# A feed-forward pass with its products five steps ahead, loading and layer norm inside it, and every engine loop written out, in a fused transformer block

## The chip, the cores and the metric

The kernel runs on one core of one Trainium2 chip. Its time is the device time of one launch in microseconds (us), the median of three runs. The engines are named as in the profile: PE is TensorE, DVE is VectorE, ACT is ScalarE, POOL is GpSimd, SP is SyncE, which here only issues DMAs.

## The reference

x is 2 x 1024 tokens of 128 channels. Two feed-forward passes stand around one attention:

```python
def ffn(x):                                   # x is layer-normed
    scores = sigmoid(x @ gate_w) + gate_bias  # 8 experts in 4 groups
    # group score: sum of its 2 scores; keep 2 groups, then the 2 best experts in them
    w = 2.5 * chosen / (sum of the 2 chosen + 1e-20)
    experts = silu(x @ w_gate[e]) * (x @ w_up[e]) @ w_down[e]      # I = 64
    shared = silu(x @ sw_gate) * (x @ sw_up) @ sw_down             # I = 128
    return (sum of w[e] * experts[e]) + shared

def attention(x):                             # 16 heads of 8 channels
    q, k, v = split(x @ W_attn + b_attn)
    s = q k^T over all keys;  s = (s - mean(s)) / (mean(|s - mean(s)|) + 1e-6) * 4
    r = relu(causally masked s) ** 4
    return (r / (sum(r) + 1e-6) @ v) @ W_proj + b_proj

x = x + 0.5 * ffn(layernorm(x))
x = x + attention(layernorm(x))
return x + 0.5 * ffn(layernorm(x))
```

## The kernel before, in words

Tokens are cut into 16 tiles of 128, four spans of 512 (four tiles each). The stages follow one another as blocks, with all engines meeting between blocks: loading x with its statistics (`load_x`), first feed-forward pass ("f1"), q, k and v, attention, its merge, and the second pass ("f2"). Inside a block each engine has its own list of instructions, in the order in which the Python code issues them, and runs it strictly in that order; semaphores (`wait_ge`, `then_inc`) tie the lists together. No scheduler moves anything.

A feed-forward pass (`ffn`) holds its hidden layer with hidden channels on the partitions. The eight experts are four chunks of two experts each (128 hidden channels); the shared expert is a fifth. So each of the four spans has five chunks, in the order 0 to 3 and then the shared one. One chunk is: on TensorE the gate product (line 463) and the up product (467), 128 x 512 each; on ScalarE silu of the gate product (588); on VectorE their product (689, `product`), into one of three `hid` buffers; on TensorE the spreading of the token's expert weights over the hidden channels (474, `spread`), which the shared chunk doesn't have; on VectorE the scaling with them (717); on TensorE the down product (446, `down`), which adds five chunks up in one PSUM bank. Gate, up and spread have two PSUM buffers each. In a span TensorE issues for chunk c: products of c, spread of c, down of c-1. After the span ScalarE takes the sum out (573), TensorE turns it back (455, four transposes), VectorE adds it to x (`add_to_x`, 697) and, in f1, takes the statistics for the next norm (310, 319).

Ahead of this stands the routing. TensorE turns the normed x (387), multiplies with the router weights (508, `logits`, two spans at a time), ScalarE takes the sigmoid (557), TensorE turns the scores (519), VectorE adds the bias (643, `scores`) and works out the two experts of each token by counting better ones: `pick_groups` (652 to 662), `pick_experts` (to 669), `weigh` (673 to 681), which ends in `parts`, three bf16 parts of each weight. They are done for span 0 alone first (`now`), and for spans 1 to 3 (`later`) between the chunks of span 0. TensorE turns `parts` (482) and ScalarE takes them as `wT` (577), which `spread` reads. ScalarE loads another function table between sigmoid and silu. Span 0 is written out; spans 1 to 3 are a hardware loop (`Fori`, from line 543 on TensorE).

In f1 the norm of all 16 tiles is one step (`norm_vector`, tiles at 351; every fourth tile on ScalarE, 366), and GpSimd prepares constants for the attention (`attention_constants`, large memsets) beside it. In f2 the first two spans are normed before the block.

The attention runs through eight "quads". Quads 0 and 7 are written out and quads 1 to 6 are a hardware loop over three pairs (`quads`, line 980), on all engines. In a quad TensorE fills a PSUM bank with scores (1048), VectorE masks (1136) or sums (1144), ScalarE and GpSimd (1206) square.

## Time and profile before

| | us |
|---|---|
| median of 3 runs | 505.78 (505.57 to 507.81) |
| span of the profiled execution, whose own time is some 0.4 more (505.8) | 505.4 |
| loading x and statistics | 0 to 9.4 |
| first feed-forward pass | 9.7 to 92.5 |
| q, k, v | 92.7 to 118 |
| attention | 118 to 406 |
| merge | 406 to 431 |
| second feed-forward pass | 431.1 to 502.6 |
| last stores | to 505.4 |
| PE / DVE / ACT / POOL busy | 441.9 (87%) / 402.7 (80%) / 342.0 (68%) / 243.8 (48%) |

A row of a timeline has the start, the duration, the engine, the line of the kernel, the operation with what it writes and reads, how many such instructions stand together, and in brackets how long the engine had been idle and what it waited for. In a row of a chain the first number is the time, the second how much of the chain that step takes. A row of the view by stretches has the stretch, its length, and then the busy time (with the number of instructions) of PE, PEld, DVE, ACT and POOL.

### The profile page before, as it was taken

How to read it: one execution, taken by the hardware profiler on the slowest of the kernel's cores; microseconds unless marked ns; L12 is line 12 of the kernel's file. 1: busy time of each engine (PE TensorE's matmuls, PEld its weight loads, DVE VectorE, ACT ScalarE, POOL GpSimd, SP SyncE). 2: the span in 40 equal slices, each digit the busy share in tenths (PEclk: the TensorE clock that was granted, in tenths of full speed). 3: DMA queues.
4: the chain of work that ended last, by engine and by line, in shares of the span. 5: the costliest groups of instructions: out<-in, count | busy, mean ns of one | idle time of the engine just before them, and what ended most of it. 6: DMA issues, size and time to landing. Idle time of an engine off the chain costs nothing. (4 is left out here: it accounts for less than half of the span.)

```text
span 505.4 us, 8943 instructions
## 1 busy us (share of the span) xinstructions
PE 441.9 (87%) x2736; PEld 168.3 (33%) x2736; DVE 402.7 (80%) x832; ACT 342.0 (68%) x576; POOL 243.8 (48%) x180
## 2 busy tenths in 40 slices
PE   0879999664799999999999999999999995879996
PEld 0323444431232332333333322323323354334442
DVE  5884556976898998999989899989988969784443
ACT  3413223554999999999999999999989931523221
POOL 5940000333777686776877677676876720000000
PEclk9979999975999999999999999999999998799999
DMA  4300000025714205105114124043002300000001
GB/s 118 75 1 0 1 0 0 6 65 127 208 33 78 60 1 95 43 1 93 42 30 71 34 51 84 0 72 63 0 0 50 85 12 0 1 1 0 21 21 42
DMA packets 17796, 21.32 MB, mean 42 GB/s; under 512 B 4748, under 2 KB 10476, under 8 KB 17772
## 3 DMA queue, kind: packets, MB, share of 16 engines
q1 hardware_dynamic: 17452, 20.95, 19.2%
q8 instruction: 12, 0.20, 0.2%
q10 hardware_dynamic: 320, 0.07, 0.1%
q14 instruction: 12, 0.10, 0.1%
HBM read 13.02 MB, written 7.86 MB: 41 GB/s over the span
## 5 line engine op out<-in xcount | busy, mean ns | idle before, releaser
L1206 POOL TENSOR_TENSOR arena<-arena 128x1024 f32<-128x1024 f32 (+1 forms) x120 | 204.0, 1722 | 63.7 <-ACT arena L1178 63.5
L1136 DVE SCALAR_TENSOR_TENSOR arena<-bank,masks 128x1024 f32<-128x1024 f32 (+1 forms) x160 | 174.9, 1114 | 28.9 <-PE bank L1048 28.6
L1178 ACT ACTIVATE arena<-arena 128x1024 f32<-128x1024 f32 (+1 forms) x160 | 148.5, 961 | 8.8 <-DVE arena L1136 5.8
L1048 PE MATMUL bank<-Q,K 128*128 128x512 bf16 (+3 forms) x384 | 91.4, 334 | 10.6 <-DMA K<-k_parts 9.2
L1048 PE MATMUL bank<-K,Q 128*128 128x512 bf16 (+3 forms) x384 | 90.4, 331 | 11.6 <-DVE arena L1136 11.5
L1144 DVE TENSOR_SCALAR_CACHE_REDUCE bank<-bank 128x128 f32<-128x128 f32 (+7 forms) x128 | 94.8, 772 | 0.0
L1168 ACT ACTIVATE bank<-bank 128x128 f32<-128x128 f32 (+7 forms) x128 | 80.9, 632 | 8.9 <-PE bank L1048 8.6
L1079 PE MATMUL bank<-arena,Vq 128*32 128x512 f32 (+3 forms) x768 | 79.6, 495 | 0.0
L588 ACT ACTIVATE arena<-bank 128x512 f32<-128x512 f32 x40 | 23.9, 597 | 76.5 <-PE bank L463 76.5
L689 DVE TENSOR_TENSOR arena<-arena,bank 128x512 f32<-128x512 f32 x40 | 27.4, 686 | 42.8 <-PE bank L467 42.7
L1079 PE MATMUL bank<-arena,ones_rows 128*32 128x512 f32 (+3 forms) x640 | 61.1, 473 | 0.0
L1048 PEld LDWEIGHTS bank<-Q,K 128*128 128x128 bf16 x384 | 26.4, 98 | 95.8 <-issue 42.2
L1048 PEld LDWEIGHTS bank<-K,Q 128*128 128x128 bf16 x384 | 32.5, 98 | 46.3 <-DVE arena L1136 28.1
L446 PE MATMUL bank<-arena,WD 128*128 128x512 f32 x80 | 42.8, 617 | 2.7 <-DVE arena L717 2.6
L463 PE MATMUL bank<-xnT,WG 128*128 (+1 forms) x80 | 42.4, 612 | 2.0 <-ACT arena L577 2.0
L467 PE MATMUL bank<-xnT,WU 128*128 (+1 forms) x80 | 41.7, 604 | 0.0
L1182 ACT ACTIVATE arena<-arena 128x1024 f32<-128x1024 f32 (+1 forms) x40 | 38.9, 972 | 1.3
L917 POOL TENSOR_TENSOR X<-X,bp 128x2048 f32<-128x2048 f32 x1 | 4.5, 4533 | 63.8 <-DVE arena L351 63.8
L1079 PEld LDWEIGHTS bank<-arena,Vq 128*32 128x32 f32 x768 | 17.3, 108 | 35.5 <-issue 34.3
L717 DVE TENSOR_TENSOR arena<-arena,bank 128x512 f32<-128x512 f32 x32 | 22.0, 688 | 5.4 <-PE bank L474 2.2
L1079 PEld LDWEIGHTS bank<-arena,ones_rows 128*32 128x32 f32 x640 | 15.5, 108 | 30.4 <-issue 30.1
L1168 ACT ACTIVATION_READ_ACCUMULATOR bank<-bank (+1 forms) x128 | 23.6, 184 | 0.0
(122 smaller groups left out, 355.4 us busy)
## 6 DMA issues: line engine op xcount, KB each, us to landing
Q<-q_parts SPq DMA_DIRECT2D x24, 192.0 KB
att<-arena SPq DMA_DIRECT2D x28, 128.0 KB, 2.0
K<-k_parts SPq DMA_DIRECT2D x16, 128.0 KB
K<-k_parts SPq DMA_DIRECT2D x8, 192.0 KB
X<-in_L_attn_x SPq DMA_DIRECT2D x4, 256.0 KB, 4.6
K<-k_parts SPq DMA_DIRECT2D x16, 64.0 KB
out_x<-X SPq DMA_DIRECT2D x4, 256.0 KB, 2.3
q_parts<-arena SPq DMA_DIRECT2D x3, 256.0 KB
```

What stands on the lines that cost most here:

```text
L446: mm = nc.tensor.matmul(down_ps, m.WD[:, c, :], hid[:, HID[c], :], start=(c == 0), stop=(c == NCH))
L463: nc.tensor.matmul(gate_ps[c % 2], m.WG[:, c * P:(c + 1) * P], x, start=True, stop=True)\
L467: nc.tensor.matmul(up_ps[c % 2], m.WU[:, c * P:(c + 1) * P], x, start=True, stop=True)\
L689: nc.vector.tensor_tensor(hid[:, HID[c], :], silu[:, c % 2, :], up_ps[c % 2], ALU.mult)\
L1048: last = nc.tensor.matmul(bank[:, lo + shift:hi + shift], left[par][:, g, blk * P:(blk + 1) * P], right[par][:, g, s0:s0 + hi - lo], start ...
L1079: mm = nc.tensor.matmul(acc[32 * g:32 * (g + 1), s0:s0 + hi - lo], w, src, start=start, stop=stop, skip_group_check=True)
L1136: nc.vector.scalar_tensor_tensor(Y(r, g)[:, lo - off(r):hi - off(r)], tiles[slot["lower", r, g]][:, lo:hi], 0.0, mask, ALU.max, ALU.mult). ...
L1144: last = nc.vector.tensor_scalar(src, src, 0.0, 0.0, ALU.max, ALU.add, accum_out=m.upper[:, blk, bass.ds(q * G + g + N_HEAD, 1)])
L1168: last = nc.scalar.activation(src, src, ACT.Relu, accum_out=m.upper[:, blk, bass.ds(q * G + g + N_HEAD, 1)])
L1178: nc.scalar.activation(z, Y(r, g)[:, tile_low(r) - off(r):T - off(r)], ACT.Square)\
L1182: nc.scalar.activation(z, z, ACT.Square).then_inc(fourth_a, 1)
L1206: nc.gpsimd.tensor_tensor(z, z, z, ALU.mult).then_inc(fourth_p, 1)
```

## The change

In both feed-forward passes the shared chunk comes first (ORDER), products run five chunks ahead (AHEAD) into six `hid` buffers, and the first five products are woven into the routing. All 20 chunks are written out. In f1, loading and statistics of x go into the block of the pass; the norm goes span by span; the weights' DMAs stand right behind those of x; GpSimd's attention constants wait for all routing weights. In the attention the loop over quads becomes plain Python, that is straight code.

```diff
+AHEAD, NHID = 5, 6
+ORDER = [NCH, 0, 1, 2, 3]
...
             logits(0)
+            products(0)
             for i in HALVES[1]:
                 norm_transpose(nc, m, s, pe, i)
             turn_scores(0)
+            products(1)
             logits(1)
-            products(0, 0, False)
+            products(2)
             turn_scores(1)
-            products(0, 1, False)
+            products(3)
+            products(4)
             pe.wait_ge(parts_ready, 1)
             turn_weights(0)
             pe.wait_ge(wT_ready, 1)
-            span(0, True)
-            pe.wait_ge(wT_ready, NSPAN)
-            with pe.Fori(1, NSPAN) as i:
-                span(i, False)
-            down(NSPAN - 1, NCH, False)
-            turn_back(NSPAN)
+            for n in range(LAST):                 # 20 chunks
+                if n == 4:
+                    pe.wait_ge(parts_ready, 2)
+                    for j in range(1, NSPAN):
+                        turn_weights(j)
+                    pe.wait_ge(wT_ready, NSPAN)
+                if routed(n):
+                    spread(n)
+                if n + AHEAD < LAST:
+                    products(n + AHEAD)
+                if n and not routed(n):
+                    turn_back(span_of(n) - 1)
+                down(n)
...
         @block.scalar                             # after sigmoid(1)
+            for n in range(AHEAD):
+                gate(n)
+            act.wait_ge(wT_zeroed, 1)
+            take_weights(0)
+            for n in range(LAST):
+                if n == 4:
+                    for j in range(1, NSPAN):
+                        take_weights(j)
+                if n and not routed(n):
+                    take_out(span_of(n) - 1)
+                if n + AHEAD < LAST:
+                    gate(n + AHEAD)
+                if following is not None and n == LAST - AHEAD - 1:
+                    nc.scalar.activation(m.table[:, :], m.eps[:, :], ACT.Sqrt)
+                    act.wait_ge(following.moments_ready, 1)
+                    norm_root(nc, m, following, act, 0)
...
         @block.gpsimd
             if beside is not None:
-                pool.wait_ge(wT_zeroed, 1)
+                pool.wait_ge(parts_ready, 2)
                 beside(nc, m, sem, pool)
...
         @block.vector
+            if start is not None:                 # f1
+                start.moments(dve, 0, s)
+                for i in range(NSPAN):
+                    if i + 1 < NSPAN:
+                        start.moments(dve, i + 1, s)
+                    norm_vector(nc, m, s, dve, i)
             scores(0)
             pick_groups(now)
+            product(0)
             pick_experts(now)
+            product(1)
             scores(1)
             weigh(now)
-            product(0, 0)
+            for n in range(2, AHEAD):
+                product(n)
+            for n in range(LAST):
+                if routed(n):
+                    scale(n)
+                # pick_groups, pick_experts, weigh of `later` at n = 0, 1, 2
+                if n + AHEAD < LAST:
+                    product(n + AHEAD)
+                if place_of(n) == 1 and n > 1:
+                    add_to_x(span_of(n) - 1)      # f1: statistics and moments with it
...
     def quads(engine, body):
-        body(0, 0, 1)
-        with engine.Fori(0, NQUAD // 2 - 1) as pair:
-            body(2 * pair + 1, 1, pair + 1)
-            body(2 * pair + 2, 0, pair + 2)
-        body(NQUAD - 1, 1, NQUAD // 2)
+        for q in range(NQUAD):
+            body(q, q % 2, q // 2 + 1)
```

TensorE at the start of the first pass; L387 (now L408) turns x, L508 (L524) is `logits`, L519 (L535) `turn_scores`, L463 and L467 (L472, L476) the products, L482 the turning of the weights. Before:

```order
L387 MATMUL bank<-ident,arena 128x128 x8
L508 MATMUL bank<-xnT,gw 32x512 x2
L387 MATMUL bank<-ident,arena 128x128 x8
L519 MATMUL bank<-ident,arena 128x64 x4
L508 MATMUL bank<-xnT,gw 32x512 x2
L463 MATMUL bank<-xnT,WG 128x512
L467 MATMUL bank<-xnT,WU 128x512
L519 MATMUL bank<-ident,arena 128x64 x4
```

And now:

```order
L408 MATMUL bank<-ident,arena 128x128 x8
L524 MATMUL bank<-xnT,gw 32x512 x2
L472 MATMUL bank<-xnT,WG 128x512
L476 MATMUL bank<-xnT,WU 128x512
L408 MATMUL bank<-ident,arena 128x128 x8
L535 MATMUL bank<-ident,arena 128x64 x4
L472 MATMUL bank<-xnT,WG 128x512
L476 MATMUL bank<-xnT,WU 128x512
L524 MATMUL bank<-xnT,gw 32x512 x2
```

Two chunks' products stand ahead of the second half of the logits, where none stood; f2 has the same rows but for the first eight transposes.

TensorE at the end of the second pass, with waits; L474 (L484) is `spread`, L446 (L499) `down`, L455 (L509) the turning back. Before:

```order
L463 MATMUL bank<-xnT,WG 128x512 [waits f2_silu]
L467 MATMUL bank<-xnT,WU 128x512 [waits f2_prod]
L443 REGISTER_ALU
L446 MATMUL bank<-arena,WD 128x512 [waits f2_hid]
L543 REGISTER_ALU
L543 COMPARE_AND_BRANCH
L446 MATMUL bank<-arena,WD 128x512 [waits f2_prod]
L455 MATMUL bank<-ident,arena 128x128 [waits f2_y]
```

And now:

```order
L499 MATMUL bank<-arena,WD 128x512 [waits f2_y,f2_prod]
L484 MATMUL bank<-arena,sel 128x512 [waits f2_scaled]
L499 MATMUL bank<-arena,WD 128x512 [waits f2_scaled]
L484 MATMUL bank<-arena,sel 128x512 [waits f2_scaled]
L499 MATMUL bank<-arena,WD 128x512 [waits f2_scaled]
L484 MATMUL bank<-arena,sel 128x512 [waits f2_scaled]
L499 MATMUL bank<-arena,WD 128x512 [waits f2_scaled]
L484 MATMUL bank<-arena,sel 128x512 [waits f2_scaled]
L499 MATMUL bank<-arena,WD 128x512 [waits f2_scaled]
L509 MATMUL bank<-ident,arena 128x128 [waits f2_x,f2_y]
```

The last chunks' products have moved away to places five chunks earlier; spread and down alternate.

VectorE in the attention, where quads 1 to 6 begin, with waits; L1136 (L1186) is the mask step. Before:

```order
L1136 SCALAR_TENSOR_TENSOR arena<-bank,masks 128x512 [waits lower_ready]
L1144 TENSOR_SCALAR bank,upper<-bank 128x512 [waits upper_ready]
L1136 SCALAR_TENSOR_TENSOR arena<-bank,masks 128x512 [waits lower_ready] x2
L1144 TENSOR_SCALAR bank,upper<-bank 128x512 [waits upper_ready]
L984 UNCONDITIONAL_BRANCH
L984 ISA
L1130 ISA [waits relu_round_summed]
L1134 ISA [waits square_done]
L1136 SCALAR_TENSOR_TENSOR arena<-bank,masks 128x1024 [waits lower_ready]
L1130 REGISTER_ALU [waits relu_round_summed]
L1134 REGISTER_ALU [waits square_done]
```

And now:

```order
L1186 SCALAR_TENSOR_TENSOR arena<-bank,masks 128x512 [waits lower_ready] x2
L1194 TENSOR_SCALAR bank,upper<-bank 128x512 [waits upper_ready]
L1186 SCALAR_TENSOR_TENSOR arena<-bank,masks 128x1024 [waits lower_ready,square_done,relu_round_summed] x2
L1194 TENSOR_SCALAR bank,upper<-bank 128x1024 [waits upper_ready]
L1186 SCALAR_TENSOR_TENSOR arena<-bank,masks 128x1024 [waits lower_ready,square_done,relu_round_summed] x2
```

The waits that stood in register instructions of their own have moved onto the instruction, as quad 7 already had them.

## Rows read from the trace of the kernel before

**Rows 1.** Head of the page
```profile
span 505.4 us, 8943 instructions
```

**Rows 2.** Chain that ended last, in order of time, one chunk and the turn back (start, us, what)
```profile
488.07 0.86 PE bank L463 x2
...
489.78 0.22 PE bank L474
490.00 0.86 PE bank L446 x2
490.86 0.44 PE bank L455 x4
```

**Rows 3.** Busy time by stretch: us, busy (x count) per engine, PEclk, DMA share, GB/s
```profile
25.00:30.00 5.00, 2.52 (x10) 0.90 (x10) 3.83 (x12) 1.38 (x3) 4.80 (x16) 1.00 0.00 2
30.00:35.00 5.00, 4.37 (x7) 1.85 (x6) 4.58 (x23) 0.18 (x1) 1.43 (x5) 0.52 0.00 0
```

**Rows 4.** Timeline of the first feed-forward pass (start us, us, engine line op out<-in)
```profile
3.80 0.87 DVE L310 BATCH_NORM_STATS2 stats<-X 128x6 f32<-128x128 f32 x4 [3.80 <-DMA X<-in_L_attn_x]
...
10.41 9.95 DVE L351 TENSOR_SCALAR arena<-X,mv,arena 128x128 f32<-128x128 f32 x12
...
21.38 0.29 DVE L643 TENSOR_TENSOR arena<-bank,gb 128x32 f32<-128x32 f32 x2 [1.02 <-PE bank L519]
```

**Rows 5.** Timeline, start of the second feed-forward pass
```profile
431.11 1.92 PE L508 MATMUL bank<-xnT,gw 128*32 128x512 f32 x4 [3.62 <-PEq L992]
...
435.59 0.29 DVE L643 TENSOR_TENSOR arena<-bank,gb 128x32 f32<-128x32 f32 x2 [2.22 <-PE bank L519]
...
437.08 0.59 ACT L557 ACTIVATE arena<-bank 64x512 f32<-64x512 f32 x1 [1.51 <-PE bank L508]
437.26 0.21 DVE L652 TENSOR_TENSOR arena<-arena 128x28 f32<-128x28 f32 x1
...
438.99 0.60 ACT L588 ACTIVATE arena<-bank 128x512 f32<-128x512 f32 x1
...
439.47 0.29 DVE L643 TENSOR_TENSOR arena<-bank,gb 128x32 f32<-128x32 f32 x2 [0.25 <-PE bank L519]
...
441.56 0.39 PE L482 MATMUL bank<-identb,arena 128*24 128x128 bf16 x4 [0.29 <-DVE arena L681]
...
442.69 0.61 PE L474 MATMUL bank<-arena,sel 128*128 128x512 bf16 x2 [0.74 <-ACT arena L577]
443.19 0.69 DVE L717 TENSOR_TENSOR arena<-arena,bank 128x512 f32<-128x512 f32 x1 [1.08 <-PE bank L474]
...
443.93 1.12 PE L446 MATMUL bank<-arena,WD 128*128 128x512 f32 x2 [0.63 <-DVE arena L717]
...
454.50 1.82 ACT L577 ACTIVATE arena<-bank 24x512 bf16<-24x512 bf16 x3 [0.59 <-PE bank L482]
```

**Rows 6.** Timeline, end of the second feed-forward pass
```profile
500.61 0.60 ACT L573 ACTIVATE arena<-bank 128x512 f32<-128x512 f32 x1 [2.24 <-PE bank L446]
```

**Rows 7.** Timeline of the first pass: TensorE at its loop's start, VectorE's last operation
```profile
44.93 1.12 PE L463 MATMUL bank<-xnT,WG 128*128 x2 [1.11 <-ACT arena L577]
...
92.07 0.38 DVE L319 BATCH_NORM_AGGREGATE mv<-stats 128x2 f32<-128x6 f32 x4
```

**Rows 8.** GpSimd's round-4 squares in quads 4, 5, 6 and 7
```profile
297.02 3.04 POOL L1206 TENSOR_TENSOR arena<-arena 128x512 f32<-128x512 f32 x3 [1.04 <-ACT arena L1178]
...
332.61 3.04 POOL L1206 TENSOR_TENSOR arena<-arena 128x512 f32<-128x512 f32 x3 [1.04 <-ACT arena L1178]
...
368.21 3.04 POOL L1206 TENSOR_TENSOR arena<-arena 128x512 f32<-128x512 f32 x3 [1.04 <-ACT arena L1178]
...
404.26 3.03 POOL L1206 TENSOR_TENSOR arena<-arena 128x512 f32<-128x512 f32 x3 [1.09 <-ACT arena L1178]
```

**Rows 9.** VectorE, the mask step that waits for the same fill, quads 6 and 7
```profile
350.45 1.23 DVE L1136 SCALAR_TENSOR_TENSOR arena<-bank,masks 128x1024 f32<-128x1024 f32 x1 [0.44 <-PE bank L1048]
...
386.39 1.23 DVE L1136 SCALAR_TENSOR_TENSOR arena<-bank,masks 128x1024 f32<-128x1024 f32 x1 [0.54 <-PE bank L1048]
```

More of the change, by code:

```diff
@@ L348, in norm_vector, with norm_tiles @@
         .then_inc(s.rstd_ready, 1)
-    for t in range(t.start, t.stop):
+def norm_tiles(nc, m, s, dve, first, last):
+    for t in range(first, last):
         if t % TPS < TPS - 1:
@@ L388, in norm_transpose, with ffn @@
     last.then_inc(s.xt_ready, 1)
-def ffn(nc, m, sem, tag, beside=None, load=None, following=None, out=None, s=None):
+AHEAD, NHID = 5, 6
+ORDER = [NCH, 0, 1, 2, 3]
+def ffn(nc, m, sem, tag, s, start=None, load=None, beside=None, following=None, out=None):
     a = Arena(m)
     b = m.psum
-    normed = NSPAN // B if s is not None else 0
-    s = s or layer_norm(nc, m, sem, tag, a, [b[0][:, 0:SPAN], b[1][:, 0:SPAN]])
-    part = len(s.parts) - 1
+    normed = 0 if start is not None else NSPAN // B
     tile8 = lambda k=E: a.take(NT * k).rearrange("p (n e) -> p n e", n=NT)
@@ L484, in turn_weights @@
                 last.then_inc(wt_ready, 1)
-            def span(i, first):
-                for c in range(HCH):
-                    again = not first or c >= 2
-                    if again:
-                        products(i, c, True)
-                    if c < NCH:
-                        spread(i, c, again)
-                    if first and c == 4:
-                        pe.wait_ge(parts_ready, 2)
-                        for j in range(1, NSPAN):
-                            turn_weights(j)
-                    if c >= 1:
-                        down(i, c - 1, first)
-                    elif not first:
-                        down(i - 1, NCH, False)
-                    if c == 1 and not first:
-                        turn_back(i)
             def logits(half):
@@ L550, in _ @@
                     norm_transpose(nc, m, following, pe, i)
+            turn_back(NSPAN - 1)
         @block.scalar
@@ L605, in _ @@
                     norm_last_tile(nc, m, following, act, i)
+            take_out(NSPAN - 1)
+            if following is not None:
                 for i in range(NSPAN // B):
                     norm_take(nc, m, following, act, i)
-        if load is not None:
+        if start is not None:
             @block.sync
             def _(sp):
+                start.sync(sp)
                 load(sp)
@@ L709, in span @@
-            def span(i, first):
-                for c in range(HCH):
-                    h = hid[:, HID[c], :]
-                    if not (first and c == 0):
-                        product(i, c)
-                    if c < NCH:
-                        dve.wait_ge(prod_ready, i * HCH + c + 1)
-                        dve.wait_ge(spread_ready, i * NCH + c + 1)
-                        nc.vector.tensor_tensor(h, h, spread_ps[c % 2], ALU.mult).then_inc(hid_ready, 1)
-                    if first and c == 0:
-                        pick_groups(later)
-                    if first and c == 1:
-                        pick_experts(later)
-                    if first and c == 2:
-                        weigh(later)
-                    if c == 2 and not first:
-                        add_to_x(i)
@@ L727, in _ @@
-            span(0, True)
-            with dve.Fori(1, NSPAN) as i:
-                span(i, False)
-            if following is not None:
-                for n in range(NSPAN // B):
-                    last = span_moments(nc, m, dve, n, stats_ready)
-                last.then_inc(following.moments_ready, 1)
-                for n in range(NSPAN // B, NSPAN - 1):
-                    span_moments(nc, m, dve, n, stats_ready)
-                norm_vector(nc, m, following, dve, 0)
-            add_to_x(NSPAN)
@@ L738, in _ @@
-            if out is None:
-                span_moments(nc, m, dve, NSPAN - 1, stats_ready)
+            for n in range(2, AHEAD):
+                product(n)
+            for n in range(LAST):
+                if routed(n):
+                    scale(n)
+                if n == 0:
+                    pick_groups(later)
+                if n == 1:
+                    pick_experts(later)
+                if n == 2:
+                    weigh(later)
+                if n + AHEAD < LAST:
+                    product(n + AHEAD)
+                if place_of(n) == 1 and n > 1:
+                    add_to_x(span_of(n) - 1)
+                if following is not None and n == LAST - 4:
+                    norm_scales(nc, m, following, dve, 0)
+                if following is not None and n > LAST - 4:
+                    half = NSPAN // B * TPS
+                    k = n - LAST + 3
+                    norm_tiles(nc, m, following, dve, [0, 3, 6][k], [3, 6, half][k])
```

297 lines of the change are left out of this document (165 added, 132 removed).

## The prediction

> **What bounds the kernel now.** I read the head of the page first: a span of 505.4 us [rows 1]; the execution's own time is some 0.4 more, so my sum, made against the span, is as good as one against the median of 505.78. Then the chain that ended last, through the second pass. The reader is to see there that inside a span of 512 tokens only TensorE speaks: a chunk is gate and up (0.86), spread (0.22), down (0.86), and once a span the turning back (0.44) [rows 2]. Each row is one step (x2 are the two instructions of one fp32 product), so a chunk is 2.80, and 2.58 without spread. In that steady state nothing is to be gained by looking further ahead: TensorE never waits. What can be gained or lost lies at the two ends of each pass, where the timelines show waits: the routing at the start [rows 4, 5] and the last takings out [rows 6, 7]. The attention, 288 us, is another loop; of it only the code's form changes.
>
> **Second pass, start.** Before: logits(0) begin at 431.11, scores(0) 435.59, pick_experts 437.26, scores(1) 439.47, weights turned at 441.56; sigmoid(1) runs at 437.08 and silu(0) follows at 438.99 [rows 5], that is 1.32 us after the sigmoid's end: a change of function tables.
> Now gate and up of chunk 0 stand ahead of the transposes. The pass begins with TensorE at half clock (the logits took 1.92 for what later takes 1.5; the other half-clock stretch, granted 0.52, is shown in [rows 3]), and before it stayed there until 436.4. So I price chunk 0's products at 2 x 1.72 = 3.44: 433.0 to 436.5. Transposes 0.9, scores turned 0.4: scores(0) at 437.95, 2.4 later than 435.59. Then products of chunk 1 (1.72) and logits(1) (1.5) at full clock: sigmoid(1) at 441.1, 4.0 later, and silu(0) at 443.0, 4.0 later. That is what decides: VectorE's list now has product(0) ahead of pick_experts. scores(0) and pick_groups take 437.26 - 435.59 = 1.67, so VectorE is free at 439.6 and idle until product(0) can run at 443.6. Behind it are queued pick_experts (437.26 to 439.2: 1.95), product(1) (0.63), scores(1) 0.32, weigh (439.8 to 441.5: 1.7): parts at 448.2 to 448.9, against 441.5. I take 448.9: **7.4 later**. Who waits for them: TensorE with turn_weights, and before it products 3 and 4, which wait for silu buffers, which wait for VectorE's product(2), just behind weigh. With 0.35 for turning, 0.6 for taking wT, and product(2) and up(4) between, the loop over chunks begins at 451.6. By then 5 chunks' products are done.
>
> **Second pass, middle.** n = 0 to 3: 4 x 1.72 + 4 x 0.86 + 3 x 0.22 = 10.98, and some 1.3 lost behind pick_experts and weigh of the later spans, each of which holds VectorE 2 to 3 us at a time (an estimate: three spans' worth, against 1.95 and 1.7 for one, in as many instructions): 463.9. Then three turned weights (0.5) and three takings of 0.61 each, 1.82 in all [rows 5], for which the whole loop waits: 466.2. n = 4 to 14 have the full work: 11 x 2.80 minus 2 spreads (0.44) plus 2 turnings (0.88) = 31.24: 497.4. Before, the same three takings lay at 454.5 to 456.3 and three looped spans followed.
>
> **Second pass, tail.** From n = 15 on no products are left. down(15) stands behind turn_back, which waits for take_out (down 14 to its end 1.0, take 0.60 [rows 6]): 2.15 instead of 0.86, 499.6. For n = 16 to 19 TensorE has spread(n), down(n) alone, and down waits for the scaling. From the one place where before shows this naked: spread at 442.69, scaling at 443.19 for 0.69, down at 443.93 [rows 5]: 1.24, and down takes 0.86: 2.10 a chunk, where the same work costs 1.08 when covered. The second spread buffer doesn't help, since spread(n+1) is issued behind down(n). 4 x 2.10 = 8.4: last down ends at 508.0. Before take_out began at 500.61 [rows 6], so **+7.4** for the pass. Bounds: if product(0)'s wait were only 2 us long and the first products not at half clock, parts come 3.5 instead of 7.4 later: +3.5; if TensorE's pauses of over 1 us in the tail bring the clock down (TensorE stood at 0.52, the 1.2 GHz level, in the 5 us after a stretch in which it was busy 2.52 of 5 us [rows 3]), the last 8 us become up to 12: +11.
>
> **First pass.** Here something is really saved. Before, the 12 norm operations took 9.95 beside GpSimd's memsets, 0.83 each [rows 4]; the memsets move behind the routing, so I price them at 0.27 (an estimate from VectorE's other plain fp32 operations on 128 columns or so in [rows 5], 0.2 to 0.3, where GpSimd rests), and they are spread between the statistics, which begin at 3.80. VectorE then needs 4 x (0.91 + 0.29) statistics, 4 x 0.4 and 12 x 0.27: norm of span 3 is done at about 14.2 instead of 20.4. The x transfers land as before; the weights come earlier (their DMAs no longer wait for a new block), in time for gate(0) at 14.0 if they take the 4 us that they took before. logits(0) to 14.0, chunk 0's products to 15.7, transposes to 16.6, scores(0) at 17.2 against 21.38: **4.2 earlier**. Then the same in-order wait as above: sigmoid(1) 20.4, silu(0) 22.3, VectorE idle 4 us, parts at 28.1, where the casts of weigh (0.6 beside GpSimd) now cost 0.2. Before, parts were ready at 28.6. So of the 4.2 only 0.5 is left at this point. The loop begins at 30.9; n = 0 to 3 with later routing and taking of weights to 45.4. Before, at 44.93 TensorE began span 1 [rows 7]; now it has products 0 to 8 and downs 0 to 3 done at 45.4: the same work short of one spread. n = 4 to 14: 31.24 and twice 0.82, since statistics (0.92 + 0.33) stand ahead of the next scaling on VectorE: 78.3. n = 15: take_out stands behind silu(19), a table load and a root on ScalarE, 81.2. n = 16 to 19: 2.1, 3.0 (statistics and norm scales in front), 2.1, 2.1: 90.4 (with some 0.1 rounding). Take out, turn, add, statistics, moments: 94.0, against 92.45 [rows 7]: **+1.6**.
> TensorE's clock: before, it was granted 0.52 from 30 to 35 behind the thin stretch 25 to 30 [rows 3], and the 44.93 has that in it. My steps from 14.0 on are all at 2.4 GHz, and TensorE now has a pause of its own from 20.2 to 22.9. If half clock follows, 5 us of it do 2.6 us of work and cost 2.4, where no wait for VectorE covers them: **+2.4**. Bounds: 0 (no such stretch, or all of it beside waits for VectorE) and 4 (a longer one).
>
> **GpSimd.** The 21 us of constants now run beside n = 3 to 11 of f1; VectorE's operations there read PSUM, and its one routing piece left, weigh(later), is before. Hidden; if not, 0.6 instead of 0.2 on a few operations, under 2 us. If they ended after the pass, q, k, v would wait: 41 + 21 = 62, far from 92.
>
> **Attention.** Rounds of the same kind are 35.59 apart where the loop jumps back between them (297.02 to 332.61), 35.60 where it doesn't (332.61 to 368.21), and 36.05 into quad 7, which is straight code (404.26) [rows 8]. The mask step shows where it goes: idle 0.44 before it in the loop, 0.54 in quad 7 [rows 9]; three waits on one instruction instead of two done ahead in registers. Six quads x 0.45 = **+2.7**. Bounds: 0, if quad 7 is slow for what is last about it (no next quad's loads), and 3.5, if K's loads shift as well.
> A rule against this: the Trainium skill (Runtime: NRT & Kernel Launch, section Instruction fetch mechanics) says that a taken branch breaks the sequential prefetch and that full unrolling is to be preferred. The trace of this case shows 35.59 with the jump back and 35.60 without, so the jump has no price here that its removal could give back. By the rule alone the 2.7 would be 0 or a gain; that outcome is rival 1.
>
> **Sum.** 7.4 + 1.6 + 2.4 + 2.7 = 14.1: a span of 519.5, and a time of about the same. I predict **519.5 us**.
>
> **Rivals.** (1) The straight attention costs nothing: 519.5 - 2.7 = 516.8. For it: one quad is the only witness, and it is also the last. 15%.
> (2) The clock: pauses in both tails and the idle VectorE stretch in f2 give further half-clock stretches, 3 to 6 us more: 522 to 525. For it: [rows 3]; against it, at most one such stretch in each pass before. 20%.
> (3) The front of f2 loses less (product(0) waits 2 us, full clock): 508 to 512. 10%.
> (4) Faster: five products ahead keep TensorE busy through the routing. The place is the start of the pass: before, TensorE was at span 1's start at 44.93 [rows 7] and at 456.7 in f2 with waits of some 10 us in each pass. If product(0) did not hold pick_experts (silu(0) early enough, i.e. before 440 in f2 and 19 in f1), the five products would fill those waits: f1 -8 and f2 -5, with +2.7 for the attention: 495.5. It decides for this side as soon as silu(0) comes less than 1 us after pick_groups ends. Against it: sigmoid(1) and the table load stand ahead of silu(0) on ScalarE, and logits(1) ahead of that on TensorE behind two products. 10%.
> The forecast itself has 45%, its own range 515 to 522.
>
> Under 0.5% (2.5 us) nothing can be told from no change here. Faster: 0.10; same: 0.02; slower: 0.88. The range that leaves out no more than 2 in 10 reaches from 508 to 525.
>
> **What would show it.** Right: in f2 an idle stretch of VectorE of about 4 us between pick_groups and product(0), ended by ScalarE's silu; weights turned at about 449; four spreads at 2.1 us intervals at the end; 36.0 us between quads. In f1 norm operations of 0.27 and scores(0) at about 17. Wrong: a product(0) that starts right behind pick_groups, spreads 1.1 apart in the tail, or quads still 35.6 apart. If the weights' DMAs behind x land after 17 us, f1's start is later and the sum for it too low.

## The result

The changed kernel takes 528.50 us (median of 4 runs, 527.78 to 528.98) against 506.17: a ratio of 1.0436 (1.0414 to 1.0458). It is slower by 22 us. I had predicted slower, 519.5, within 508 to 525: the direction was right, and the time lies 3.5 us outside the range. One execution of x4 below (1472.51 us) and one of x12 (515.0) were slow ones: they stand in no ratio, though the medians below count them.

The page of the profile after has the span:

```profile
span 526.9 us, 7795 instructions
```

It is 21.5 longer than before [rows 1]. These executions took 1.9 to 2.0 us more than their span. The table ahead of the prediction puts this difference at 0.4 for the kernel before; in every execution of it for which both are on record it is 1.8 to 1.9, and those with a span of about 505.4 took 507.0 to 507.4. So 519.5 as a span would have been some 521.4 as a time, an estimate from these differences: of the 9.0 us by which the time was missed, about 2 lie there and 7 in the span. Where the 21.5 arise, by the start of the same operation in both timelines:

| stage | before | after | change |
|---|---|---|---|
| to the first matmul of q, k, v | 92.76 | 99.83 | +7.1 |
| q, k, v, to the first copy of V | 25.6 | 24.9 | -0.7 |
| attention, first to last copy of V | 263.3 | 267.8 | +4.5 |
| to the first logits of the second pass | 49.5 | 49.2 | -0.3 |
| second pass, to its last addition | 70.8 | 81.8 | +10.9 |

**First pass, start** (the timeline, as in [rows 4]):

```profile
11.89 0.85 DVE L372 TENSOR_SCALAR arena<-X,mv,arena 128x128 f32<-128x128 f32 x3
...
18.10 0.29 DVE L684 TENSOR_TENSOR arena<-bank,gb 128x32 f32<-128x32 f32 x2 [4.30 <-PE bank L535]
...
21.54 1.28 ACT L623 ACT_TABLE_LOAD   x1
22.83 1.08 ACT L623 ACTIVATE arena<-bank 128x512 f32<-128x512 f32 x2
...
23.52 0.69 DVE L731 TENSOR_TENSOR arena<-arena,bank 128x512 f32<-128x512 f32 x1 [3.79 <-issue]
```

Three norm operations take 0.85, 0.28 each, where twelve took 9.95. scores(0) come 3.3 us earlier. And then VectorE stands idle for 3.79 us in front of product(0), behind a sigmoid, a table load and silu. TensorE turns the weights at 30.99, later than the 28.62 of the kernel before.

**First pass, tail** (TensorE's timeline, and the busy time by stretches):

```profile
83.49 1.12 PE L499 MATMUL bank<-arena,WD 128*128 128x512 f32 x2 [0.85 <-DVE arena L740]
...
86.30 2.07 PE L499 MATMUL bank<-arena,WD 128*128 128x512 f32 x2 [1.47 <-DVE arena L740]
...
89.65 2.08 PE L499 MATMUL bank<-arena,WD 128*128 128x512 f32 x2 [0.85 <-DVE arena L740]
...
93.00 2.07 PE L499 MATMUL bank<-arena,WD 128*128 128x512 f32 x2 [0.85 <-DVE arena L740]
```

```profile
90.00:100.00 10.00, 6.44 (x18) 3.24 (x18) 3.15 (x13) 1.99 (x4) 0.00 (x0) 0.67 0.00 0
```

The last four downs start 2.81, 3.35 and 3.35 apart. A down that took 1.12 takes 2.07, at a granted clock of 0.67 in these ten us (PEclk, the third number from the row's end) and of 0.81 in the ten before: the engine was at 1.2 GHz from 86 to 96.5. In [rows 3] such a stretch lay in the routing; in the tail the kernel before had none.

**Second pass, start** (the timeline, as in [rows 5]):

```profile
441.69 1.92 PE L524 MATMUL bank<-xnT,gw 128*32 128x512 f32 x4 [3.62 <-PEq L1042]
...
449.03 0.29 DVE L684 TENSOR_TENSOR arena<-bank,gb 128x32 f32<-128x32 f32 x2 [5.08 <-PE bank L535]
...
453.84 1.08 ACT L623 ACTIVATE arena<-bank 128x512 f32<-128x512 f32 x2
...
454.53 0.69 DVE L731 TENSOR_TENSOR arena<-arena,bank 128x512 f32<-128x512 f32 x1 [3.87 <-issue]
...
462.27 0.39 PE L516 MATMUL bank<-identb,arena 128*24 128x128 bf16 x4
```

Counted from the first logits, scores(0) start at 7.3 (before 4.5), silu(0) at 12.2 (7.9), the weights are turned at 20.6 (10.5). VectorE's idle stretch before product(0) is 3.87 us.

**Second pass, tail** (the chain that ended last, as in [rows 2]):

```profile
513.33 0.23 PE bank L484
...
513.65 0.70 DVE arena L740
...
514.39 1.12 PE bank L499 x2
515.52 0.23 PE bank L484
```

Before, this chain held only TensorE. Now it goes spread, VectorE's scaling (the "DVE arena L740" rows), down, 2.19 us a chunk. The tail had the full clock here. Both kernels began the pass at 1.2 GHz, this one until 6.3 us after the first logits, the one before until 5.3; this one had two more stretches with less than the full clock:

```profile
454.00:464.00 10.00, 8.77 (x22) 3.31 (x23) 7.63 (x38) 3.31 (x6) 0.00 (x0) 0.83 0.00 1
474.00:484.00 10.00, 7.98 (x27) 3.13 (x26) 2.76 (x5) 3.69 (x7) 0.00 (x0) 0.83 0.00 0
```

**Attention** (GpSimd's squares, as in [rows 8], and VectorE's mask step, as in [rows 9]):

```profile
307.04 3.04 POOL L1256 TENSOR_TENSOR arena<-arena 128x512 f32<-128x512 f32 x3 [1.08 <-ACT arena L1228]
...
343.06 3.04 POOL L1256 TENSOR_TENSOR arena<-arena 128x512 f32<-128x512 f32 x3 [1.08 <-ACT arena L1228]
...
379.09 3.04 POOL L1256 TENSOR_TENSOR arena<-arena 128x512 f32<-128x512 f32 x3 [1.08 <-ACT arena L1228]
```

```profile
361.23 1.23 DVE L1186 SCALAR_TENSOR_TENSOR arena<-bank,masks 128x1024 f32<-128x1024 f32 x1 [0.54 <-PE bank L1098]
```

Quads are 36.02 and 36.03 apart instead of 35.59 and 35.60, and the idle time before the mask step is 0.54, what [rows 9] had only in quad 7.

### The profile page after: what moved, and what is told of

Same layout as the page of the kernel before. It is cut to its first block and busy times, and to the rows that moved or that the text cites. A ratio compares the mean times of both kernels' runs of the same rounds, so it can differ in the third digit from the quotient of the medians.

```text
span 526.9 us, 7795 instructions
## 1 busy us (share of the span) xinstructions
PE 449.2 (85%) x2691; PEld 169.4 (32%) x2736; DVE 394.0 (75%) x838; ACT 344.4 (65%) x579; POOL 243.6 (46%) x180
## 5 line engine op out<-in xcount | busy, mean ns | idle before, releaser
L1186 DVE SCALAR_TENSOR_TENSOR arena<-bank,masks 128x1024 f32<-128x1024 f32 (+1 forms) x160 | 175.0, 1114 | 32.7 <-PE bank L1098 31.2
L1098 PE MATMUL bank<-Q,K 128*128 128x512 bf16 (+3 forms) x352 | 88.3, 329 | 15.4 <-DMA K<-k_parts 11.6
L499 PE MATMUL bank<-arena,WD 128*128 128x512 f32 x80 | 45.6, 653 | 9.9 <-DVE arena L740 9.7
L472 PE MATMUL bank<-xnT,WG 128*128 128x512 f32 x80 | 44.7, 643 | 7.0 <-ACT arena L623 5.2
L476 PE MATMUL bank<-xnT,WU 128*128 128x512 f32 x80 | 44.2, 636 | 0.0
L740 DVE TENSOR_TENSOR arena<-arena,bank 128x512 f32<-128x512 f32 x32 | 21.9, 684 | 28.3 <-PE bank L484 24.6
L499 PEld LDWEIGHTS bank<-arena,WD 128*128 128x128 f32 x80 | 14.5, 202 | 31.9 <-DVE arena L740 22.3
L1218 ACT ACTIVATION_READ_ACCUMULATOR bank<-bank 128x1 f32 x128 | 23.5, 183 | 0.0
```

Source lines behind the costliest of these rows:

```text
L472: nc.tensor.matmul(gate_ps[n % 2], m.WG[:, c * P:(c + 1) * P], x, start=True, stop=True)\
L476: nc.tensor.matmul(up_ps[n % 2], m.WU[:, c * P:(c + 1) * P], x, start=True, stop=True)\
L499: nc.tensor.matmul(down_ps, m.WD[:, chunk_of(n), :], hid[:, n % NHID, :], start=(place == 0), stop=(place == HCH - 1)).then_inc(down_read, 1)
L1098: last = nc.tensor.matmul(bank[:, lo + shift:hi + shift], left[par][:, g, blk * P:(blk + 1) * P], right[par][:, g, s0:s0 + hi - lo], start ...
L1186: nc.vector.scalar_tensor_tensor(Y(r, g)[:, lo - off(r):hi - off(r)], tiles[slot["lower", r, g]][:, lo:hi], 0.0, mask, ALU.max, ALU.mult). ...
L1218: last = nc.scalar.activation(src, src, ACT.Relu, accum_out=m.upper[:, blk, bass.ds(q * G + g + N_HEAD, 1)])
```

## The experiments

Each was timed beside runs of the kernel before on the same chip, in four rounds: x1 to x4, x5 to x8, x9 to x11, and x12. The kernel before had medians of 506.41, 507.16, 505.55 and 506.99 us in them. So kernels of different rounds are to be compared by their ratios; a difference of their medians is uncertain by 1 to 2 us. Stages are read from one profiled execution of each kernel.

| kernel | median us | ratio to before (95%) |
|---|---|---|
| x1 straight attention only | 509.04 | 1.0057 (1.0039 to 1.0075) |
| x3 the same, waits split | 505.47 | 0.9982 (0.9967 to 0.9998) |
| x12 as x1, the late wait written first | 505.37 | 0.9968 (0.9955 to 0.9981) |
| x2 changed kernel, looped attention | 524.77 | 1.0356 (1.0304 to 1.0407) |
| x4 and spread ahead in the tail | 511.39 | 1.0072 (1.0035 to 1.0110) |
| x5 x2 with the routing first | 517.56 | 1.0219 (1.0180 to 1.0257) |
| x6 x2 with filler in the tail | 520.22 | 1.0249 (1.0216 to 1.0282) |
| x7 x4 and x5 together | 504.14 | 0.9946 (0.9925 to 0.9966) |
| x8 x7 with straight attention, waits split | 503.05 | 0.9930 (0.9904 to 0.9956) |
| x9 x8, two ahead in the second pass | 503.25 | 0.9944 (0.9921 to 0.9967) |
| x11 x8, three ahead in both | 504.14 | 0.9961 (0.9935 to 0.9988) |
| x10 x8, GpSimd's constants early | 509.85 | 1.0064 (1.0043 to 1.0085) |

### The attention: x1, x3, x12, x2

```diff
 # x1: the kernel before
-        body(0, 0, 1)
-        with engine.Fori(0, NQUAD // 2 - 1) as pair:
-            body(2 * pair + 1, 1, pair + 1)
-            body(2 * pair + 2, 0, pair + 2)
-        body(NQUAD - 1, 1, NQUAD // 2)
+        for q in range(NQUAD):
+            body(q, q % 2, q // 2 + 1)
 # x3: x1 and, on VectorE
                         dve.wait_ge(relu_summed, ...)
                         dve.wait_ge(square_done, ...)
+                        dve.sem_inc(ahead, 1)
                         dve.wait_ge(lower_ready, ...)
 # x12: x1 and
+                    dve.wait_ge(lower_ready, ...)
                     if r in (2, 3) or not first_quad(q):
                         dve.wait_ge(relu_summed, ...)
                         dve.wait_ge(square_done, ...)
-                    dve.wait_ge(lower_ready, ...)
```

x1: 

> The kernel before with one edit: the attention's eight quads written out instead of looped. Theory A (straight code costs each of quads 1 to 6 some 0.43 us, read off the changed kernel, where quads are 36.03 apart against 35.60): 6 x 0.43 = 2.6 more, quads 36.0 apart, the first quad unchanged, so 508.4 (0.5% slower). Rival B (the 0.43 comes from something else in the changed kernel, such as where its buffers or constants lie): quads 35.6 apart and 505.8, no difference. Rival C (a taken branch costs and straight code saves it): under 505.

x3: 

> As the one before (straight attention, nothing else), but on VectorE the waits for square_done and relu_round_summed stand on a semaphore increment of their own ahead of each mask step, so that the mask step itself waits for lower_ready alone, as in the loop. Theory A1 (three waits on one instruction make it start 0.1 us late, 0.54 against 0.44 idle before it): the idle time is 0.44 again, quads come back to about 35.7, total 506.2. Rival A2 (straight code as such is fetched or decoded later, the waits don't matter): still 36.0 or more, 508.4 to 509, since an instruction is added per mask step.

x12: 

> As x1 (the kernel before with straight attention, 509.0), with the same three waits of the mask step in another order in the code: lower_ready, which comes last, is now written first. Theory A3 (an instruction of VectorE carries only part of three waits; the rest goes to an inserted semaphore instruction, in x1's trace one of 50 ns that ends at the wait for lower_ready, 0.095 us ahead of each mask step; what costs is that the semaphore that comes last is on the inserted one): the inserted instruction is done early, the idle time is 0.44, quads 35.6 apart, 505 to 506.5. Rival A4 (three waits cost 0.1 us in whatever order): 0.54, quads 36.03 apart, 509.

x2: 

> The changed kernel with one edit undone: the attention is a loop again as before. Theory A: quads 35.6 apart, 2.6 to 4.5 us less than the changed kernel's 528.5: 524 to 526. Whether the first quad's extra 1.6 us stays tells whether it belongs to the straight code (then 524.0) or to the low clock and the later transfers around it (525.6). Rival B: 528.5 as the changed kernel.

The same mask step in VectorE's timeline, x1, then x3, then x12:

```profile
352.26 1.23 DVE L1133 SCALAR_TENSOR_TENSOR arena<-bank,masks 128x1024 f32<-128x1024 f32 x1 [0.54 <-PE bank L1045]
```

```profile
350.23 1.23 DVE L1135 SCALAR_TENSOR_TENSOR arena<-bank,masks 128x1024 f32<-128x1024 f32 x1 [0.44 <-PE bank L1045]
```

```profile
351.29 1.22 DVE L1133 SCALAR_TENSOR_TENSOR arena<-bank,masks 128x1024 f32<-128x1024 f32 x1 [0.44 <-PE bank L1045]
```

In the trace's full list of records (start us, ns, operation), which the timeline leaves out, a semaphore instruction stands before this step, in x1 and in x12:

```
352.161   50 EVENT_SEMAPHORE          349.126 1665 EVENT_SEMAPHORE
352.256 1225 SCALAR_TENSOR_TENSOR     351.289 1224 SCALAR_TENSOR_TENSOR
```

x1 is slower by 0.57% (2.9 us), with quads 36.03 apart, and nothing else is changed: theory A holds, B and C fall. In x3 the code is as straight as in x1 and has an instruction more at each of these steps; the idle time is 0.44 again and the quads are 35.60 apart. Three waits on one instruction (A1) were a good name for it, but not the right one: x12 waits for the same three semaphores on the same instruction, and has 0.44 and quads 35.59 apart. It is A3: of three waits a part goes to an inserted instruction. In x1 that one carries the wait that ends last (the list of records has each wait's semaphore), and the mask step starts 0.095 us after its start, 0.045 after its end. In x12 the inserted one is over early, and the mask step itself waits for TensorE. The Trainium skill (Perfetto Trace Analysis, section Identifying Dependency Chains) says that an instruction that waits on several engines may have such instructions inserted before it; the trace agrees. Straight code as such costs nothing: x12, straight and with that one line moved, is 0.3% under the kernel before. In quad 7 and in the first one the kernel before had mask steps with 0.54 too, and x12 has none there. x2 is 3.7 under the changed kernel, within what A gives. The time from the first to the second copy of V, which holds the first quad, is 49.6 before, 51.2 in the changed kernel and in x1, 49.7 in x3, 50.6 in x12 and 50.4 in x2, and 50.1 to 50.9 in the kernels below: the waits may have a part in its extra 1.6, and what sets the rest was not tried.

### The tail: x4, x6

```diff
 # x4: x2 and
-                if routed(n):
+                if routed(n) and n < LAST - AHEAD:
                     spread(n)
                 if n + AHEAD < LAST:
                     products(n + AHEAD)
+                elif n + 1 < LAST:
+                    spread(n + 1)
 # x6: x2 and
+                elif routed(n):
+                    if n == LAST - NCH:
+                        pe.wait_ge(silu_ready, LAST)
+                    nc.tensor.matmul(gate_ps[0], m.WG[:, 0:P], m.xnT[:, (NSPAN - 1) * SPAN:],
+                                     start=True, stop=True)
```

x4: 

> Looped attention (as in the run before), and in both passes' last five chunks, where no products are left, spread(n+1) is issued ahead of down(n). Theory T (the tail is a chain spread, scale, down of 2.2 us a chunk because spread(n+1) stands behind down(n)): chunks of about 1.1 instead of 2.19 in the second pass, 3 to 4 of them: 3.5 to 4.5 us less there; in the first pass, whose tail ran at half clock with 3.35 a chunk, 4 to 9 less. Total 513 to 517. Rival U (the tail is bound by the clock or by VectorE's scaling, not by the order on TensorE): less than 2 us gained, 523 to 525.

x6: 

> The changed kernel with looped attention (524.8), and in the last four chunks of both passes one more gate product of 0.86 us between spread and down, whose result nobody reads; it fits into the 1.02 us in which TensorE waits for the scaling. Theory K (the pauses in the tail bring the clock to 1.2 GHz, which makes a chunk of the first pass's tail 3.35 instead of 2.19): the four chunks are 2.2 each and no stretch at 0.5 lies in the tail, 3.5 us less in the first pass, up to 2 in the second: 519 to 521, although TensorE does more. Rival L (the clock falls for another reason, or the filler only delays down): 525 to 528.

x4 is 13.4 under x2, more than I expected (511.4 against 513 to 517). TensorE's timeline in the first pass's tail:

```profile
81.12 1.02 PE L499 MATMUL bank<-arena,WD 128*128 128x512 f32 x2
81.98 0.38 PE L484 MATMUL bank<-arena,sel 128*128 128x512 bf16 x1
82.20 1.02 PE L499 MATMUL bank<-arena,WD 128*128 128x512 f32 x2
...
84.28 1.12 PE L499 MATMUL bank<-arena,WD 128*128 128x512 f32 x2 [0.84 <-DVE arena L742]
...
85.64 2.23 PE L499 MATMUL bank<-arena,WD 128*128 128x512 f32 x4
```

Downs are 1.08 apart (the last row holds two) but for one that waits behind the statistics; q, k, v start at 91.94 instead of 99.44. The second pass takes 75.99 instead of 81.66; x2's tail ran at 1.2 GHz there too (below), so x4's gain holds the pauses and the clock in both passes. Two spread buffers let the scaling of the next chunk run beside down, with no other instruction added.

x6 does more work on TensorE and is 4.6 us faster. The same tail there, L572 being the filler:

```profile
81.39 0.38 PE L484 MATMUL bank<-arena,sel 128*128 128x512 bf16 x1
81.60 1.02 PE L572 MATMUL bank<-xnT,WG 128*128 128x512 f32 x2
82.62 1.13 PE L499 MATMUL bank<-arena,WD 128*128 128x512 f32 x2
...
85.42 1.13 PE L499 MATMUL bank<-arena,WD 128*128 128x512 f32 x2 [0.61 <-DVE arena L744]
...
87.61 1.13 PE L499 MATMUL bank<-arena,WD 128*128 128x512 f32 x2
...
89.81 1.13 PE L499 MATMUL bank<-arena,WD 128*128 128x512 f32 x2
```

```profile
80.00:90.00 10.00, 9.36 (x25) 3.69 (x26) 6.30 (x21) 0.88 (x2) 0.00 (x0) 1.00 0.00 0
```

Each down takes 1.13 and chunks are 2.19 apart (2.80 with the statistics), at a granted clock of 1.00, where x2 had 3.35; q, k, v start at 94.99, 4.45 earlier. 0.6 of that is there already when the tail begins (span 2 is turned back at 80.03 against 80.64), so the tail gives 3.8: that is what the low clock cost there. Theory L falls.

Theory K holds in part. All four executions of x6 had a higher mean granted clock (0.960 to 0.969) than three of the four of x2 (0.950 or 0.951; the fourth had 0.961). But the pauses don't always bring the clock down. x5, which comes next, has the same pauses in this tail and no filler, and its downs are just as short and as far apart:

```profile
84.64 1.13 PE L499 MATMUL bank<-arena,WD 128*128 128x512 f32 x2 [0.85 <-DVE arena L738]
...
86.84 1.12 PE L499 MATMUL bank<-arena,WD 128*128 128x512 f32 x2 [0.85 <-DVE arena L738]
```

From the turning back of span 2 to q, k, v it takes 14.96 us, as in x6, and x2 takes 18.80. Of the six tails with these pauses, in the changed kernel, x2 and x5, four had a stretch at 1.2 GHz; of x6's two none had. That the filler keeps the clock up is likely by this, not shown.

The second pass took as long in both (81.69 and 81.66), but not for want of a gain in its tail: from its down of n = 15 to the last addition x6 takes 11.2 and x2 13.6, which ran at 1.2 GHz there. x6 had lost as much before: that down comes 70.5 after the first logits against 68.1, behind longer stretches at 1.2 GHz at the start.

### The start: x5

```diff
             logits(0)
-            products(0)
             for i in HALVES[1]: norm_transpose(...)
             turn_scores(0)
-            products(1)
             logits(1)
-            products(2)
+            products(0)
             turn_scores(1)
-            products(3)
-            products(4)
+            products(1)
             pe.wait_ge(parts_ready, 1)
-            pe.wait_ge(s.xnT_ready, NSPAN)
             turn_weights(0)
+            for n in range(2, AHEAD):
+                products(n)
 # VectorE: pick_experts, scores(1), weigh, and then product(0) to product(4)
```

x5: 

> The changed kernel with looped attention (524.8) and the old order at the start of both passes: on TensorE logits(1) ahead of the first products, products 2 to 4 behind the turned weights; on VectorE pick_experts, scores(1) and weigh ahead of all five products. Five products ahead are kept. Theory F (product(0) in front of pick_experts holds the routing back): VectorE's idle stretch of 3.9 us is gone, weights are turned 6 to 8 us earlier, products 2 to 4 (5.2 us) lie behind them and scalings of later spans start behind more products: 4 to 6 us less in each pass, 513 to 517. Rival G (TensorE has the same work either way and only the place of its pauses moves): 2 us less or nothing, 522 to 525.

x5 is 7.2 under x2 (6.9 by the ratios); 517.6 is 0.6 above what theory F gave, and 4 below what G gave. The wait that is gone in front of `turn_weights` is one that `logits(1)` has already made. The start of the second pass:

```profile
430.35 1.05 PE L524 MATMUL bank<-xnT,gw 128*32 128x512 f32 x4 [2.27 <-PEq L1041]
...
434.57 0.29 DVE L682 TENSOR_TENSOR arena<-bank,gb 128x32 f32<-128x32 f32 x2 [1.97 <-PE bank L535]
...
436.55 0.59 ACT L581 ACTIVATE arena<-bank 64x512 f32<-64x512 f32 x1 [2.00 <-PE bank L524]
...
438.49 0.60 ACT L621 ACTIVATE arena<-bank 128x512 f32<-128x512 f32 x1
...
439.81 0.29 DVE L682 TENSOR_TENSOR arena<-bank,gb 128x32 f32<-128x32 f32 x2 [1.61 <-PE bank L535]
...
441.91 0.40 PE L516 MATMUL bank<-identb,arena 128*24 128x128 bf16 x4 [0.29 <-DVE arena L720]
```

The weights are turned 11.6 us after the first logits (18.2 in x2, 10.5 before), and in the first pass at 22.22 instead of 30.71. In the profiled execution, the fastest of x5's four, the first pass gave 7.4 us: 3.6 of them were there when the tail began, and 3.8 are the tail at full clock. The second gave 2.2: 3.3 when its tail began, and 1.1 went again, since x5 stood at 1.2 GHz through more of that tail than x2. First x5, then x2:

```profile
500.00:510.00 10.00, 7.39 (x12) 2.02 (x10) 1.56 (x3) 0.60 (x1) 0.00 (x0) 0.50 0.00 0
```

```profile
510.00:520.00 10.00, 6.79 (x12) 2.02 (x12) 2.07 (x3) 0.60 (x1) 0.00 (x0) 0.62 0.02 5
```

So the reordered start is worth 3.3 to 3.6 us a pass here, less than F's 4 to 6, and the clock in the tails gives or takes as much.

### All together: x7, x8

x7: 

> The changed kernel with all three put right: looped attention, spread one ahead in the tail (511.4 with these two), and the routing first at the start of both passes. Theory F adds its 4 to 6 us a pass: 500 to 504, under the kernel before (506.4), since loading and norm in one block save some 4 us of the first pass. Rival G: 509 to 511.5.

x8: 

> As x7 with the attention as straight code whose mask step has the two early waits on a semaphore increment of its own. By the comparison made on the kernel before (505.5 against 506.4) 0 to 1 us less than x7: 499.5 to 504. If the gain there was chance: the same as x7.

The edits add up within the noise: 13.4 of x4 and 7.2 of x5 make 20.6, and x7 is 20.6 under x2. Against x4, where neither tail has these pauses, the routing first gives 3.9 us in the first pass (q, k, v at 88.00 against 91.94) and 4.4 in the second (71.60 against 75.99). It beats the kernel before by 0.5%, x8 by 0.7% (the two intervals overlap, so that x8 is the better one isn't shown). The gain is in the first pass, as in the timeline of x7:

```profile
7.01 0.85 DVE L372 TENSOR_SCALAR arena<-X,mv,arena 128x128 f32<-128x128 f32 x3
...
12.51 0.85 DVE L372 TENSOR_SCALAR arena<-X,mv,arena 128x128 f32<-128x128 f32 x3
...
16.05 0.29 DVE L684 TENSOR_TENSOR arena<-bank,gb 128x32 f32<-128x32 f32 x2 [2.69 <-PE bank L535]
...
21.84 0.39 PE L516 MATMUL bank<-identb,arena 128*24 128x128 bf16 x4 [0.29 <-DVE arena L722]
```

q, k, v start at 88.00 against 92.76. The second pass takes 71.60 against 70.84 before: there the reordered kernel gains nothing even with all repairs.

### How far ahead, and the constants: x9, x11, x10

```diff
 # x9: x8 and
+    AHEAD = 5 if tag == "f1" else 2
 # x9 and x11
-                if routed(n) and n < LAST - AHEAD:
+                if routed(n) and n <= LAST - AHEAD:
 # x11: x8 and
-AHEAD, NHID = 5, 6
+AHEAD, NHID = 3, 4
 # x10: x8 and
-                pool.wait_ge(parts_ready, 2)
+                pool.wait_ge(wT_zeroed, 1)
```

x9: 

> As x8 (503.05, ratio 0.993 to the kernel before), with products only two chunks ahead in the second pass; the first pass keeps five. Theory H (TensorE has no pause in the spans' steady state, so looking further ahead than two gives nothing, and its three more chunks of products only put off the first down and leave a longer tail without products): the second pass takes 70.5 to 71.5 from its first logits to its last addition, against 71.85 in x8 and 70.84 before: 502 to 503. Rival J (the five products cover the routing of the later spans): 2 to 4 us more, 505 to 507.

x11: 

> As x8 with three chunks ahead (four hid buffers) in both passes. Theory H: the second pass 70.5 to 71.9; in the first pass the same start, 0 to 1 us more at its end, where statistics and norm of the next stage now lie between fewer products: 502 to 504. Rival J: 505 to 507.

x10: 

> As x8, but GpSimd's attention constants start right behind the clearing of wT, as in the kernel before, instead of behind the routing weights: they then lie beside norm and routing. Theory M (GpSimd's memsets are what made a norm operation 0.83 instead of 0.28 us before): norm operations of some 0.8 for the later spans, scores(0) 2 to 4 us later than 16.1, weights turned 3 to 6 us later than 21.9, 3 to 5 us more in all: 506 to 508. Rival N (moving them is worth nothing; the norm is short because it goes span by span): 503.

With five ahead, both conditions of `spread` pick the same chunks. x9 and x11 can't be told from x8 by their times (intervals overlap), as theory H says; its figures for the stages held only in part: x9's second pass took 73.3 in the profiled execution, the slowest of its six (expected 70.5 to 71.5), x11's 71.2, and x11's first pass ended 1.8 later than x8's. J's 2 to 4 us are not seen: by the ratios x9 lies 0.7 and x11 1.6 us above x8, but with these intervals up to 2.5 and 3.4 us are not excluded. How much of such differences of 1 to 2 us in one execution is the place of the half-clock stretches is open.

x10 loses 6.8 us on x8, more than theory M's 3 to 5. VectorE's timeline there:

```profile
10.56 3.08 DVE L372 TENSOR_SCALAR arena<-X,mv,arena 128x128 f32<-128x128 f32 x3
...
14.27 4.93 DVE L372 TENSOR_SCALAR arena<-X,mv,arena 128x128 f32<-128x128 f32 x3
...
19.34 0.93 DVE L372 TENSOR_SCALAR arena<-X,mv,arena 128x128 f32<-128x128 f32 x3
21.74 0.29 DVE L684 TENSOR_TENSOR arena<-bank,gb 128x32 f32<-128x32 f32 x2 [1.47 <-PE bank L535]
```

Three norm operations beside the memsets take 3.08 and 4.93, so up to 1.6 us each, and 0.31 when they are over. scores(0) come 5.6 later, the weights at 29.87 instead of 21.89, and q, k, v start 9.65 later. This was x10's slowest execution (512.64 us), with the granted clock at 0.66 from 20 to 30, where x8 had the full one; so the 9.65 are more than the 6.8 of the medians. Rival N falls. This one moved wait carries more than the whole gain of x8, 0.7% or 3.5 us.

## Why the prediction was wrong

The order of its steps held: what I said would show it right stood in the profile, an idle stretch of about 4 us before product(0) (3.79 and 3.87), downs about 2.1 apart in the tail (2.19), 36.0 between quads, norm operations of 0.28. The sum was 14.1 and the span grew by 21.5; that a time was put equal to its span (see the result) adds about 2 to the miss.

- **The clock term was mis-sized; this is the step that failed.** I put 2.4 us once, for a stretch in the first pass's routing, and left the tails at 2.4 GHz, although the bounds of the second pass's tail had named it and rival (2) gave 522 to 525 with 20%. In the changed kernel the stretch in the routing was shorter, from 24.8 to 28.2, and cost at most 1.7 (half of its length, an estimate). The tail, where the sum had nothing, ran at 0.81 from 80 to 90 and at 0.67 from 90 to 100, and that cost 3.8: the same tail takes that much less at full clock, with filler in x6 and without it in x5. The second pass had two stretches of ten us at 0.83; each costs at most 0.17 x 10 = 1.7, an estimate. Without the 3.8 the time would have been 528.5 - 3.8 = 524.7, an estimate, inside the range. The tail of the second pass, which I feared for, ran at full clock in this execution, and at half in x2's and x5's, whose order of work there is the same: that it happens is shown, what decides it isn't.
- **First pass: +7.1 for +4.0.** scores(0) at 18.1 for 17.2, the loop at 32.1 for 30.9, spread(4) at 46.8 for 45.4: 1.4 behind by then, where the 2.4 of the clock were meant to come on top. Then the tail: the last down ends at 95.1 for 90.4, and most of that is the clock.
- **Second pass: +10.9 for +7.4.** silu(0) 4.3 later for 4.0; weights turned 20.6 after the first logits for some 18, the loop over chunks at 21.7 for 20.5. The tail's chunks were 2.19 for 2.10. What remains of the 3.5 is of the size of the two stretches, which is all that is known of it.
- **Attention: +4.5 for +2.7.** The six quads gave 5 x 0.43 + 0.33 = 2.5, as forecast but for 0.2. My reason, three waits on one instruction, was half right: x12 has them and doesn't pay; what counts is whether the one that ends last is written first. What I missed: one of the six intervals was 36.38 (0.35 more), and the first quad took 1.6 longer, for a reason that stays open.
- **Loading, norm and GpSimd's constants.** The 4.2 us at scores(0) were 3.3. I had called the move of the constants hidden and priced only the norm; x10 gives it 6.8 us, measured on x8 and not on the changed kernel. It was in my sum through the 0.27, so it isn't an error of the sum, but I didn't see how much hung on it.
- **The rivals.** (1) fell with x1: straight code with the waits as written does cost. The advice for full unrolling (the Trainium skill, Runtime: NRT & Kernel Launch, section Instruction fetch mechanics) comes out better than I had weighed it: straight with the waits in the right order, x12 and x3 stand at 0.9968 and 0.9982 of the looped kernel, although the quads of both are as far apart as in the loop. The order of the waits in quads 0 and 7, which the kernel before had straight already, is another candidate for the 0.2 to 0.3% that they save, so no gain from the missing branches is shown. (4), the faster one, fell as its own condition said: silu(0) started 3.2 us after pick_groups had ended, not under 1. With the routing first and the tail mended, x7 is in fact faster, 504.1, but not by the 10 us of that rival: in the second pass five products ahead found nothing to fill.

## What to carry to other kernels

In this kernel, look-ahead in a loop that already kept its bounding engine busy moved the pauses to the ends: there the last items need an order of their own (the next item's small first step ahead of this item's last), and nothing of the bulk work may stand in front of the chain that releases the start. Before pricing such a pause by its length, price the clock that may follow it: from the down of n = 15 to q, k, v it took 18.3 us in x2, 14.5 with the pauses at full clock (x5) and 10.8 without them (x4). And where an instruction of VectorE waits for several semaphores, as the mask step does here, write the one that comes last first in the code, and look in the trace which wait an inserted instruction carries.

## What was not expected of the hardware

- Of three waits of a VectorE instruction a part is done by an inserted instruction. When that one ends last, VectorE is idle for 0.54 us before the step, otherwise for 0.44 (x1 and x12): 0.43 us a quad, and a ratio of 1.0057 against 0.9968 for the order of three lines.
- The same tail, with the same pauses of 0.85 and 1.47 us, took 3.8 us more when TensorE fell to 1.2 GHz in it (18.80 in x2, 14.96 in x5), and of six such tails in three kernels four had such a fall. A matmul more per chunk was no loss: x6, with its tails at a granted clock of 1.00, is 4.6 us faster than x2.
- A plain fp32 VectorE operation of 128 x 128 took 0.28 alone and up to 1.6 beside GpSimd's memsets (x10), where the kernel before had shown 0.83.
